# Statistics of the first layer normalisation moved from a preparing stage into the attention loop, their roots from ScalarE and VectorE to GpSimd

## The reference

```python
x = x + tanh(g_xattn) * cross_attention(layernorm(x), ctx)      # 8 heads of 64
x = x + tanh(g_ffn) * moe(layernorm(x))                         # 16 experts, top 2, and a shared one
def layernorm(x): return (x - mean(x)) / sqrt(var(x) + 1e-5)    # over the 256 features
```

## Time and profile before

| | us |
|---|---|
| median of three runs | 1044.93 (1041.34 to 1046.5) |
| the profiled execution | 1043.86 |
| its span | 1041.7 |
| TensorE busy | 909.5 (87%) |
| VectorE busy | 804.5 (77%) |
| ScalarE busy | 478.8 (46%) |
| GpSimd busy | 475.1 (46%) |

### The profile page before, as it was taken

The page is one execution under the profiler, slowest core; times in us unless marked ns, Lnnn a source line. Parts: engine busy times, 40 slices in busy tenths (PEclk is TensorE's granted clock), DMA queues, the critical chain, the costliest instruction groups (busy, mean ns, idle before and its releaser), DMA issues. The chain is left out here.

```text
span 1041.7 us, 22369 instructions
## 1 busy us (share of the span) xinstructions
PE 909.5 (87%) x6728; PEld 857.2 (82%) x6729; DVE 804.5 (77%) x1837; ACT 478.8 (46%) x970; POOL 475.1 (46%) x495
## 2 busy tenths in 40 slices
PE   2559999999999999999949999999565899599994
PEld 2449999999999999998847888887465899499994
DVE  5768888888898888998737898888534677467773
ACT  3345555555555555554445455543122344144441
POOL 6134434343343434334321555455415466537775
PEclk9999999999999999999968999999868899889998
DMA  8621222122221222212151444442769899488890
GB/s 216 215 87 35 80 68 67 54 57 79 66 79 45 66 66 67 68 54 67 53 172 32 173 166 160 170 170 108 275 222 318 284 341 344 146 267 260 268 289 29
DMA packets 108096, 150.64 MB, mean 145 GB/s; under 512 B 21622, under 2 KB 72186, under 8 KB 108032
## 3 DMA queue, kind: packets, MB, share of 16 engines
q1 hardware_dynamic: 92672, 107.60, 34.1%
q0 software_dynamic: 15360, 42.24, 10.6%
HBM read 90.19 MB, written 65.90 MB: 150 GB/s over the span
## 5 line engine op out<-in xcount | busy, mean ns | idle before, releaser
L549 POOL TENSOR_TENSOR prob<-prob,row_sum 128x616 f32<-128x616 f32 x64 | 77.9, 1218 | 148.7 <-DVE row_sum L739 148.7
L1364 POOL DMA_INDIRECT rows_scratch<-prow x80 | 78.7, 983 | 75.0 <-DVE prow L1500 47.2
L956 POOL DMA_INDIRECT rows_scratch<-row,slot x64 | 67.8, 1060 | 75.8 <-DVE row L1203 61.2
L1364 POOL DMA_INDIRECT out<-prow x80 | 78.7, 983 | 50.1 <-issue 26.4
L1482 DVE TENSOR_TENSOR eyT_lo<-ps_ey,eyT_hi 128x512 fp32r<-128x512 f32 x80 | 55.2, 690 | 55.6 <-ACT eyT_hi L1457 55.1
L1457 ACT ACTIVATE eyT_hi<-ps_ey 128x512 fp32r<-128x512 f32 x80 | 47.9, 599 | 109.3 <-PE ps_ey L1386 109.3
L75 PE MATMUL ps_h<-w_flat,eyT_hi 128*128 x320 | 98.1, 307 | 0.0
L224 POOL TENSOR_TENSOR xT_lo<-xT_raw,xT_hi 128x512 fp32r<-128x512 f32 x32 | 41.2, 1286 | 121.7 <-ACT ctxb_hi L190 121.6
L1386 PE MATMUL ps_ey<-ident,prow 128*128 128x128 f32 x320 | 51.6, 286 | 49.2 <-DMA prow<-rows_scratch 45.9
L190 ACT ACTIVATE M_hi<-ps_proj 128x308 f32 (+1 forms) x128 | 54.4, 429 | 84.1 <-PE ps_proj L77 84.0
L76 PE MATMUL ps_h<-w_flat,eyT_hi 128*128 x320 | 90.9, 284 | 0.0
(11 more groups left out here) (232 smaller groups left out, 3383.3 us busy)
## 6 DMA issues: line engine op xcount, KB each, us to landing
prow<-rows_scratch SPq DMA_DIRECT2D x160, 258.0 KB, 3.8
rows_scratch<-blank SPq DMA_DIRECT2D x34, 258.0 KB, 4.0
xs<-in_x SPq DMA_DIRECT2D x16, 512.0 KB, 4.5
xT_raw<-in_xT SPq DMA_DIRECT2D x32, 256.0 KB, 3.8
x_tok<-in_x SPq DMA_DIRECT2D x32, 256.0 KB, 2.9
x_scratch<-x_tok SPq DMA_DIRECT2D x32, 256.0 KB, 3.0
row<-x_scratch SPq DMA_DIRECT2D x16, 512.0 KB, 4.0
w_raw<-in_W SPq DMA_DIRECT2D x16, 256.0 KB, 3.5
```

Source lines behind the costliest of these rows:

```text
L549: nc.gpsimd.tensor_tensor(pr, pr, row_sum[i][:, :].unsqueeze(2).broadcast_to((P, H, CK)), ALU.mult).then_inc(normed, 1)
L956: pool.indirect_dma_start(c.rows1, bass.IndirectOffsetOnAxis(slot1[:, t:t + 1], 0), row[G % NX][:, i, :], None).then_inc(scattered[G % NX] ...
L1364: pool.indirect_dma_start(dram, bass.IndirectOffsetOnAxis(target, 0), row[u][:, i, 0:columns], None, bounds_check=bound, oob_is_err=False) ...
```

## The change

Statistics of the first 16 tiles (batches 0 to 7, two groups) are made in `prepare`, from three loads of 512 KB and two of 256 KB into new buffers `x_ahead`, with no buffer used twice. The other 48 tiles are loaded in `attend`: at the head of batch b SP loads x of batch b + 8 into `x_ahead[b % 2]`, and VectorE makes its two statistics at two places of batch b, groups 0 to 5. The reciprocal deviations come from GpSimd in 20 chained instructions: variance, a first guess from the bits of the float, three Newton steps. This is done once for 16 tiles as GpSimd's first work in `attend`, and then at the end of each of groups 0 to 5 for 8 tiles. ScalarE waits for it at the head of each group. `rstd_steps` stays for the second normalisation. The hardware loop over groups 1 to 5 becomes written-out code. The core of the diff (declarations of semaphores and tensors left out):

```diff
+def rstd_on_gpsimd(nc, pool, stats, rstd, var, work, chain, before):
...
+    link(g.tensor_tensor(work, stats[:, :, 1], stats[:, :, 4], ALU.subtract))
+    link(g.tensor_tensor(work, work, work, ALU.mult))
+    link(g.tensor_scalar(work, work, 0.25, LN_EPS, ALU.mult, ALU.add))
+    link(g.tensor_tensor(var, stats[:, :, 2], stats[:, :, 5], ALU.add))
+    link(g.tensor_scalar(var, var, 1.0 / D, None, ALU.mult))
+    link(g.tensor_tensor(var, var, work, ALU.add))
+    link(g.tensor_scalar(rstd.bitcast(I32), var.bitcast(I32), -0.5, float(SEED), ALU.mult, ALU.add))
+    link(g.tensor_scalar(var, var, -0.5, None, ALU.mult))
+    for _ in range(3):
+        link(g.tensor_tensor(work, rstd, rstd, ALU.mult))
+        link(g.tensor_tensor(work, work, var, ALU.mult))
+        link(g.tensor_scalar(work, work, 1.5, None, ALU.add))
+        link(g.tensor_tensor(rstd, rstd, work, ALU.mult))
...
+def load_x_ahead(sp, c, a, b, par):
+    sp.dma_start(a.x_ahead[par][:, :, :], c.x[bass.ds((b + 2 * GB) * N, N), :].rearrange("(i p) d -> p i d", p=P)
+                 ).then_inc(a.ahead_in[par], 16)
...
@@ prepare, sync
-                for n in range(TILES // 4):
-                    if n >= XB:
-                        sp.wait_ge(stats_done, 4 * (n - XB + 1))
+                for par in range(2):
+                    at = (FIRST - 4 + 2 * par) * P
+                    sp.dma_start(a.x_ahead[par][:, :, :], c.x[at:at + 2 * P, :].rearrange("(i p) d -> p i d", p=P)
+                                 ).then_inc(first_in, 16)
+                for n in range(XB):
...
@@ prepare, scalar
-                act.wait_ge(root_ready, 1)
-                nc.scalar.activation(c.rstd1[:, :], c.rstd1[:, :], ACT.Sqrt).then_inc(root_done, 1)
@@ prepare, vector
-                t = iter(range(TILES))
+                t = iter(range(FIRST))
                 for n in range(4):
-                    tile_stats(islice(t, 3))
+                    tile_stats(islice(t, 1))
                     low_K(nc, v, a, n)
-                    tile_stats(islice(t, 3))
+                    tile_stats(islice(t, 1))
                     for k in range(4):
                         low_M(nc, v, a, n, 0, n, k)
-                        tile_stats(islice(t, 2 if k < 3 else 0))
+                        tile_stats(islice(t, 1 if k % 2 == 0 else 0))
...
-                v.wait_ge(stats_done, TILES)
-                rstd_steps(nc, v, stats, mean1[:, :], c.rstd1[:, :], var1[:, :], chain1, root_ready, root_done)
+                v.wait_ge(stats_done, FIRST)
@@ attend
-            body(0, True, False)
-            with eng.Fori(1, GROUPS - 2) as g:
-                body(g, False, False)
-            body(GROUPS - 2, False, False)
-            body(GROUPS - 1, False, True)
+            for g in range(GROUPS):
+                body(g, g == 0, g == GROUPS - 1)
@@ attend, sync, at the head of batch b
+                        if exists(g + 2):
+                            wait(sp, ahead_stats, 2 * (b - 1))
+                            load_x_ahead(sp, c, a, b, par)
@@ attend, gpsimd
+                    if exists(g + 2):
+                        pool.wait_ge(ahead_stats, 2 * GB * (g + 1))
+                        rstd_of(2 * GB * (g + 2), 2 * GB, LN_STEPS * (g + 1))
+
+                rstd_of(0, 4 * GB, 0)
                 groups(pool, body)
@@ attend, scalar, at the head of a group
+                    act.wait_ge(rstd_ready, 1 if first else g)
@@ attend, vector, between low_M_units(b, g, q, i) and sums(b, i)
+                        if exists(g + 2):
+                            stats_ahead(b, 2 * g + q // 2, q % 2, i)
```

More of the change, by code:

```diff
@@ L131, in rstd_steps, with link @@
     link(nc.vector.tensor_tensor(rstd, rstd, var, ALU.mult))
+SEED = 0x5F3759DF
+LN_STEPS = 6 + 2 + 3 * 4
+def rstd_on_gpsimd(nc, pool, stats, rstd, var, work, chain, before):
+    step = [0]
+    def link(ins):
+        step[0] += 1
+        ins.then_inc(chain, 1)
+        pool.wait_ge(chain, before + step[0])
+    g = nc.gpsimd
+    link(g.tensor_tensor(work, stats[:, :, 1], stats[:, :, 4], ALU.subtract))
[11 more added lines that the diff above has]
+        link(g.tensor_tensor(rstd, rstd, work, ALU.mult))
 def attention_tensors(nc, c, ctx):
@@ L145, in attention_tensors @@
     a.x_tok = [sb(f"x_tok{i}", [P, 2, D]) for i in range(2)]
+    a.x_ahead = [sb(f"x_ahead{i}", [P, 2, D]) for i in range(2)]
+    a.stats1 = sb("stats1", [P, TILES * 6])
     a.M = [sb(f"M_{s}", [P, 2 * MPAR], F32R) for s in ("hi", "lo")]
@@ L154, in attention_tensors @@
     a.x_in = [sem(f"x_in{i}") for i in range(2)]
+    a.ahead_in = [sem(f"ahead_in{i}") for i in range(2)]
     a.ctx_hi, a.ctx_split = sem("ctx_hi"), sem("ctx_split")
@@ L288, in prepare @@
     XB = 3
+    FIRST = 4 * GB
     with ExitStack() as ctx:
@@ L336, in _ @@
                         sp.dma_start(wo_raw[:, :, :], c.Wout.rearrange("(q p) n -> p q n", p=P)).then_inc(wvo_in, 16)
[L337 to L342, removed]
+                sp.wait_ge(a.ctx_split, 1)
+                load_group(sp, c, a, 1)
+                load_x_side(sp, c, a, 0, 0)
+                load_x_side(sp, c, a, 1, 1)
+                load_x(sp, c, a, 0, 0)
             @block.gpsimd
@@ L430, in tile_stats @@
                         n = t // 4
-                        v.wait_ge(x_in[n % XB], 16 * (n // XB + 1))
-                        nc.vector.bn_stats(stats[:, t, :], xs[n % XB][:, t % 4, :]).then_inc(stats_done, 1)
-                t = iter(range(TILES))
+                        v.wait_ge(*((x_in[n], 16) if n < XB else (first_in, 32)))
+                        source = xs[n][:, t % 4, :] if n < XB else a.x_ahead[t % 4 // 2][:, t % 2, :]
+                        nc.vector.bn_stats(stats[:, t, :], source).then_inc(stats_done, 1)
+                t = iter(range(FIRST))
                 for n in range(4):
-                    tile_stats(islice(t, 3))
+                    tile_stats(islice(t, 1))
                     low_K(nc, v, a, n)
-                    tile_stats(islice(t, 3))
+                    tile_stats(islice(t, 1))
                     for k in range(4):
                         low_M(nc, v, a, n, 0, n, k)
-                        tile_stats(islice(t, 2 if k < 3 else 0))
+                        tile_stats(islice(t, 1 if k % 2 == 0 else 0))
                     if n == 0:
@@ L465, in attend @@
         OT = [sb(f"OT_{s}", [P, 4, N], F32R) for s in ("hi", "lo")]
+        var1, work1 = sb("var1", [P, 4 * GB]), sb("work1", [P, 4 * GB])
         ps_proj = a.ps_proj
@@ L550, in norm, with rstd_of @@
                                             ALU.mult).then_inc(normed, 1)
+                def rstd_of(first, tiles, before):
+                    stats = a.stats1[:, bass.ds(first * 6, tiles * 6)].rearrange("p (t s) -> p t s", s=6)
+                    rstd_on_gpsimd(nc, pool, stats, c.rstd1[:, bass.ds(first, tiles)], var1[:, 0:tiles],
+                                   work1[:, 0:tiles], rstd_chain, before)
+                    pool.sem_inc(rstd_ready, 1)
                 def body(g, first, last):
@@ L763, in low_PT, with stats_ahead @@
                         low(nc, PT_out(1, i, j), PT_out(0, i, j), PT_bank(j), PT_lo)
+                def stats_ahead(b, b_half, par, i):
+                    v.wait_ge(a.ahead_in[par], 16 * (b_half + 1))
+                    nc.vector.bn_stats(a.stats1[:, bass.ds((2 * (b + 2 * GB) + i) * 6, 6)],
+                                       a.x_ahead[par][:, i, :]).then_inc(ahead_stats, 1)
                 def body(g, first, last):
@@ L770, in body @@
                             low_M_units(b, g, q, 0)
+                        if exists(g + 2):
+                            stats_ahead(b, 2 * g + q // 2, q % 2, 0)
                         sums(b, 0)
@@ L777, in body @@
                             low_M_units(b, g, q, 1)
+                        if exists(g + 2):
+                            stats_ahead(b, 2 * g + q // 2, q % 2, 1)
                         sums(b, 1)
```

8 lines of the change are left out of this document (3 added, 5 removed).

## The result

| | before | after |
|---|---|---|
| median, us | 1045.28 (1041.34 to 1047.29, 5 runs) | 1036.49 (1036.05 to 1040.06, 5 runs) |
| the profiled execution | 1043.86 | 1036.33 |
| its span | 1041.7 | 1034.1 |

The ratio is 0.9925, 95% interval 0.9902 to 0.9948: faster, by 8.8 us where 9.9 had been forecast.

A forecast was written before the change was run, and what follows sets the result against it. TensorE was taken to bound attention; in prepare, VectorE's waits for x, M's chain and the closing statistics and root were the limits. Front -11.0 plus start +1.1 gave -9.9 us: 1035.0 us by the median, range 1031 to 1043.

The forecast's parts named there:

- Front: Prepare, up to attention's start: statistics, loads of x and the root chain removed, 11.0 us gained (6.9 to 11.8).
- M's chain: Prepare, TensorE, ScalarE and VectorE making M for four head pairs: ends 4.1 us earlier, 0.7 from the first K half.
- the wait for x in pair 1: Prepare, VectorE's longest wait for tiles of x (3.3 us) disappears: interval 10.72 becomes 8.15, 2.6 us gained.
- each pair's statistics: Prepare: about 0.2 us of statistics per pair stand ahead of a half TensorE waits for, 0.8 us gained in four.
- the tail from the last low half of M to the first scores: End of prepare: kT_lo no longer waits behind the statistics and root, attention starts at 55.9 instead of 62.77, 6.9 us gained.
- Start: Attention's start: ScalarE waits for GpSimd's 20 links of 0.285 us (5.7 us), 1.1 us lost; gain 0.8 to loss 4.2.
- the table load: ScalarE's 1.28 us load before the first exponential goes with the square root; were it to stay, up to 1.3 us.
- Statistics: Attention, two per batch on VectorE in 24 batches, 0.34 us each, hidden: cost 0; rival, VectorE becomes the bound, 7 us, 0.10.
- root per group: End of six groups on GpSimd: chain of 5.5 us fits in 6.6 us of room, cost 0; dear-links rival, 1051 us, 0.10.
- loop: Attention's loop written out: TensorE shows no idle, so 0; rival, hidden cost of turns, 1020 us, 0.02.
- The cover of the statistics: VectorE's waits in a batch (scores 0.37, V_hi 0.43, OT_hi 0.26 us) absorb both statistics, 0.3 us of slack left.
- Load ahead: Attention, SP's load of x issued at about 91.3 us lands in 3.8 us, before VectorE wants it: cost 0.

The follow-up runs named there:

- no_ahead_2: Changed kernel without attention's loads ahead, statistics and per-group roots, batches 8 to 31 with factors 1: 1032.0 us, 0.9872; rerun on the third chip 1091.67 us, 0.9891.
- root_load_early_2: Changed kernel with first root in prepare, second behind batch 1, loads ahead a batch earlier: 1089.23 us, 0.9835, second chip; rerun on the third 1091.59 us, 0.9895.
- unrolled: Kernel before with only attention's loop written out: 1042.34 us against 1043.55, ratio 0.9991.
- stats_kept: Changed kernel with all 64 statistics left in prepare, made from the 16 resident tiles: 1098.48 us against 1102.85, ratio 0.9965 to the kernel before.
- after_third: Changed kernel unaltered, run again on the third chip: 1091.48 us, ratio 0.9901 to the kernel before.
- long_chain: Changed kernel with five Newton steps instead of three, 28 links instead of 20: 1043.75 us, ratio 0.9995 to the kernel before.
- after_again: Changed kernel unaltered, run again on the second chip: 1091.74 us, ratio 0.9852 to the kernel before.
- root_early: Changed kernel with the first group's root made by GpSimd in prepare and the second's behind batch 1: 1091.67 us, ratio 0.9871 to the kernel before, second chip.
- wait_late: Changed kernel with ScalarE's wait for the root moved to just ahead of its first exponential: 1033.66 us, ratio 0.9896 to the kernel before.
- stats_thrice: Changed kernel with each statistic in attention made three times: 1109.25 us against 1106.7, ratio 1.0026 to the kernel before, second chip.

## Why the prediction was right, and where it wasn't

- **Front, -11.0 forecast, -13.2 in this profile, -11.1 at the lower clock.** no_ahead_2 and root_load_early_2 run the new prepare at the level that the kernel before had, but for one product, and their first scores come at 51.87 and 51.91 us where 51.8 had been forecast. The parts fit as well: M's chain ends 4.0 us earlier (4.1 forecast), by 0.6 before the first K product (0.7), 2.6 for the wait for x in pair 1 (2.6) and 0.27 for each pair's statistics (0.2); and the tail from the last low half of M to the first scores went from 12.16 to 5.07, 7.1 us (6.9). The other 2.1 us of this profile are a term that the prediction doesn't have: TensorE was granted the full clock for parts of prepare. In the three profiles with twelve statistics a pair (before, unrolled, stats_kept) no product of M's chain is at the faster pace, in nine of the eleven with four more than one is. Whether the change invites this, by shorter gaps of TensorE, or whether it is chance, no run separates.
- **Start, +1.1 forecast, +1.6 in the first batch.** The mechanism came as summed: the exponential starts 0.7 us later behind the first scores and the transposes 0.8. Two sizes were off and met: a link takes 0.31 us at 16 columns where 0.285 was taken, so the chain was 0.5 longer, and what stands between it and the exponential was 0.5 shorter; the exponential ends 8.45 us after GpSimd's first link (8.5 forecast). With the transposes at full pace the first batch is 0.9 us over the old one (after_third); in the other two profiles it is 1.6 and 1.8, and there the transposes ran at 0.50 and 0.63 of the clock. That the table load goes too was right: the tanh's load at the start of the program serves the exponential, as the Trainium skill has it (ScalarE: Activation LUTs, section on table sets).
- **Statistics, root per group, loop: 0 each.** Borne out by the batches' lengths with and without them (no_ahead_2), long_chain's bound of 6.6 us and unrolled. The cover of the statistics was read too small: V_hi's wait shrank from 0.43 to 0.29 us and the one for scores not at all, where both were to be halved.
- **Load ahead, 0 forecast.** Right as a rule (its wait on VectorE is 2.4 us in 24 batches, in three places), wrong once: 6.3 us to landing where 3.8 was taken, 0.9 us of TensorE. In the changed kernel's two other profiles no batch is long for it. root_load_early removes the wait; what made that one load late is open.
- **Tail of attention, not in the prediction.** 3.7 us of the gain were lost there in the profiled execution of the changed kernel. In all the profiles that stretch takes one of four values, whatever the kernel: 23.9 (before, long_chain, after_again, root_early, stats_kept), 25.4 (unrolled, wait_late, stats_thrice, no_ahead_2), 26.2 (no_ahead, after_third, root_load_early_2) and 27.6 us (after, root_load_early). The changed kernel itself shows three of them. The instructions are the same. In the five at 23.9 the granted clock stays at 1.00 until TensorE's last product of attention; in all others it falls in the tail, after a gap of 2.1 us in which TensorE waits for the low halves, a gap that the five have as well. What decides it is open; the kernel before shows two of the four values (23.9, and 25.4 in unrolled), so the fall isn't the change's.
- **The sum.** -13.2 + 1.6 + 0.9 + 3.7 - 0.5 = -7.5 in the two profiled executions. By cause: front -11.1, start +0.9, one late load +0.9, the clock -2.1 in prepare, +0.7 in the first batch and +3.7 in the tail, the rest -0.5. Front and start came within 0.2 us of their terms; what the prediction left out, the clock and one late load, moves single executions by some microseconds either way. That the median lies only 1.1 us from the forecast gain is in part luck.
- **Open:** on the second chip the ratio is 0.985, 15 to 16 us, while the changed kernel's `mix` begins there at 520.00, 10.8 us before the old one's 530.84 on the first chip. Where the other 5 us lie can't be said, as there is no profile of before on that chip.

## What to carry to other kernels

Before an interval that shrank is put down to an edit, look at the durations of instructions that the edit doesn't touch: here the same product took 0.46 us and then 0.30, and that explains 0.9 us of a pair's 1.2, where eight statistics taken out of the chain explain 0.27. A second profile of the same kernel tells the two apart. An experiment that is to take a wait away needs its own list of waits read: stats_kept moved one from pair 1 to pair 0, and its equal end looked like a proof. A small root can move to an idle engine as Newton steps, if the room in front of that engine's next due instruction is worked out first: here 6.6 us, and 20 links fit in it while 28 didn't.

## What the runs showed of the hardware

- GpSimd makes small chained instructions at 0.29 us each on 128x8 and 0.31 on 128x16, with 0.20 to 0.23 us for two tensors, 0.20 to 0.27 for a tensor and a scalar; arithmetic on the bits of a float as an integer costs no more (0.20 to 0.21).
- The same transposes took 1.10, 1.62 or 1.99 us, at a mean granted clock of 1.00, 0.63 and 0.50. The gap just before them doesn't decide it: behind 1.83 to 1.85 us all three occur (after_third and unrolled, after_again, after), and one kernel shows 1.10 and 1.99 behind 1.74 to 1.75 (no_ahead, no_ahead_2). One attention tail spreads over 3.7 us by the clock alone. Differences of that size between two single profiles say nothing of an edit.
- The column of the granted clock doesn't resolve the start of the program: in the windows before the first 1.00-to-0.59 step at 32 us it shows 1.00 both where a product takes 0.46 us and where it takes 0.30. There the durations tell which of the two levels (1.2 or 2.4 GHz) TensorE ran at. Likewise in the kernel before it shows 1.00 in every window up to 64 us, and every product of M's chain takes 0.46.
